# Early-fusion block on one core: one set of row statistics for two layer norms in a row, reordered attention bodies, and pair loads placed ahead of three weight loads

## The reference, cut to what matters

```python
h = tok(x)                                  # 32 images: 36 patches of 768 -> layer norm -> 192 -> layer norm, + class row
h = concat([h, txt], axis=1)                # 37 + 128 = 165 rows of 192
h = h + linear_attention(layernorm(h))      # no softmax
h = h + ffn(layernorm(h))                   # plain layer norm, then inside ffn:

def ffn(x):
    h = ln(x, g1, b1); qkv = h @ in_w.T + in_b            # a second layer norm right on the first
    x = x + softmax(q k^T / 4, 12 heads) v @ out_w.T + out_b
    x = x + gelu(x @ mlp_w1 + b1) @ mlp_w2 + b2
    xm = ln(x, g2, b2); top-2 of 4 experts by a gate; return x + weighted experts(xm)
```

## Time and profile before

| | |
|---|---|
| median of 3 runs | 1307.76 us (1306.62 to 1310.7) |
| the profiled execution, its own time | 1298.35 us |
| its span, first to last instruction | 1296.3 us |
| mean granted TensorE clock | 0.968 |
| busy: PE, DVE, ACT, POOL | 92%, 69%, 57%, 33% |
| instructions | 27864 |

### The profile page before, as it was taken

One profiled execution on the slowest core, in us unless ns is written; L12 is line 12 of the kernel. 1 busy time (PEld: TensorE's weight loads), 2 busy tenths in 40 slices (PEclk: granted clock), 3 DMA queues, 4 the chain that ended last, 5 costly groups with the idle time before them and its releaser, 6 DMA issues.

```text
span 1296.3 us, 27864 instructions
## 1 busy us (share of the span) xinstructions
PE 1191.5 (92%) x9709; PEld 1015.5 (78%) x9709; DVE 897.8 (69%) x2492; ACT 740.1 (57%) x1717; POOL 422.9 (33%) x418
## 2 busy tenths in 40 slices
PE   8885999898998999989998899999999999999994
PEld 7774777676776777777777689998988889989994
DVE  4764566766667667676667677778678876777673
ACT  4462565555655566545556665455566667667662
POOL 3511010101111010110101016787657655455544
PEclk8997999999999999999999999999999999999998
DMA  5156111212012120121220343444576767766662
GB/s 208 56 145 182 52 34 32 58 51 58 21 45 58 51 58 14 53 58 51 57 54 17 129 107 69 88 88 111 142 220 164 183 162 173 188 163 156 173 167 29
DMA packets 98554, 127.23 MB, mean 98 GB/s; under 512 B 9735, under 2 KB 90504, under 8 KB 94768
## 3 DMA queue, kind: packets, MB, share of 16 engines
q1 hardware_dynamic: 74911, 105.24, 26.9%
q0 software_dynamic: 23568, 21.06, 10.6%
HBM read 72.49 MB, written 53.72 MB: 97 GB/s over the span
## 4 chain that ended last, share of the span: by engine, by line
PE 56%; DVE 16%; issue 11%; POOL 6%; DMA 4%; SPq 3%; ACT 3%; DVEq 0%; POOLq 0%; ACTq 0%
PE PS L1863 45%; PE PS L1866 11%; DMA out<-YO,ids 3%; POOL out L891 2%; POOL expert_rows L854 2%; DVE K L1393 2%; DVE st L1293 2%; DVE XA L1304 2%; ACT GF L1177 1%; SPq L605 1%; SPq L583 1%; DVE H L1348 1%; DVE CNT L1422 1%; DVE ZS L1363 1%; DVE mv L1296 1%
## 5 line engine op out<-in xcount | busy, mean ns | idle before, releaser
L1863 PE MATMUL PS<-w2r,GH 128*120 (+1 forms) x828 | 247.6, 362 | 2.3 <-DVE GL L1588 1.1
L749 POOL TENSOR_TENSOR rs<-ve,minus_half 128x3 f32<-128x3 f32 x48 | 41.0, 854 | 535.8 <-DVE ve L1298 535.8
L891 POOL DMA_INDIRECT out<-YO,ids x94 | 162.6, 1730 | 143.7 <-DVE flag L1804 62.9
L1863 PE MATMUL PS<-w2r,GL 128*120 (+1 forms) x828 | 208.0, 251 | 0.0
L934 ACT ACTIVATE PX<-PS,nb 128x165 f32<-128x165 f32 x576 | 176.6, 416 | 39.1 <-DVE nb L1381 37.7
L1177 ACT ACTIVATE GF<-PS,b1c 128x480 f32<-128x480 f32 (+1 forms) x216 | 137.4, 637 | 82.5 <-PE PS L1863 79.7
L1863 PE MATMUL PS<-XH,w1r 128*128 128x480 f32 (+1 forms) x432 | 168.9, 393 | 6.1 <-ACT GF L1177 3.2
L1866 PE MATMUL PS<-ident,PX 128*128 128x128 f32 x864 | 136.5, 290 | 34.7 <-DVE PT L1386 27.9
L1386 DVE COPY PT<-PS 128x384 f32<-128x384 f32 x144 | 80.1, 556 | 115.0 <-PE PS L1866 114.0
L1866 PEld LDWEIGHTS PS<-ident,PX 128*128 128x128 f32 x864 | 97.3, 145 | 73.3 <-DVE PT L1386 31.5
L1863 PEld LDWEIGHTS PS<-w2r,GH 128*120 128x120 f32 x828 | 150.2, 181 | 5.7 <-DVE GL L1588 4.0
(11 more groups left out here) (292 smaller groups left out, 2327.5 us busy)
## 6 DMA issues: line engine op xcount, KB each, us to landing
w1r<-expert_w_parts SPq DMA_DIRECT2D x25, 1536.0 KB, 7.4
expert_rows<-empty SPq DMA_DIRECT2D x45, 369.4 KB, 5.6
RT<-expert_rows SPq DMA_DIRECT2D x22, 369.4 KB, 3.9
X<-x_scratch SPq DMA_DIRECT2D x11, 360.0 KB, 4.0
out<-X POOLq DMA_DIRECT2D x11, 360.0 KB, 5.6
H<-in_txt SPq DMA_DIRECT2D x16, 192.0 KB
out<-H SPq DMA_DIRECT2D x16, 192.0 KB
x_scratch<-X SPq DMA_DIRECT2D x16, 192.0 KB
```

Source lines behind the costliest of these rows:

```text
L749: nc.gpsimd.tensor_tensor(rs[:, k - 1, 0:n], ve[:, k - 1, 0:n], eps_half[:, 0:n], ALU.pow).then_inc(rstd_ready[k], 1)
L891: nc.gpsimd.indirect_dma_start(out[:, :], bass.IndirectOffsetOnAxis(ap=ids[:, i, t:t + 1], axis=0), YO[:, i % 2, t, :], None, bounds_check ...
L1863: return nc.tensor.matmul(o, l, r, start=start, stop=stop)
```

## The change

It has three parts. **Statistics**: U's own are not taken any more. `lin_out` computes two values from H1's variance v: `ve[3] = v + eps`, and `ve[4] = v (1 + eps) + eps^2`, which is (v + eps) times (v / (v + eps) + eps); POOL raises both in one instruction of six columns, and `z_out` makes Z from H1 directly, ahead of U (`u_out`). **Order**: the bodies' instructions on PE, ACT and DVE stand in a new order; the same 18 groups are copied by the same engines. **Loads**: `h1_store(1)` moves up on SP, behind `load_raw(1)`.

```diff
@@ sync @@
-        for f in range(NF):
+        load_raw(0)
+        load_raw(1)
+        sp.wait_ge(token_stored[1], 16 * (PTILES - 2))
+        h1_store(1, True)
+        for f in range(2, NF):
             load_raw(f)
...
         fill(0)
         fill(PAIRS - 2)
-        sp.wait_ge(token_stored[1], 16 * (PTILES - 2))
-        h1_store(1, True)
@@ gpsimd: rstd and body @@
+            cols = slice(k - 1, k if k == 3 else k + 1)
+            n = 3 * (cols.stop - cols.start)
...
             residual(i, first)
             if lin:
-                rstd(i + 1, 4, 3)
-                rstd(i + 1, 5, 3)
+                rstd(i + 1, 4)
@@ scalar: body @@
             exps(i, 0)
+            probsT(i, 1)
             xaT(i + 1)
             exps(i, 1)
-            probsT(i, 1)
             lin_y(i + 1, 0)
+            lin_y(i + 1, 1)
             probsT(i, 3)
             exps(i, 2)
-            lin_y(i + 1, 1)
...
             lin_m(i + 1)
+            exps(i, 4)
             probsT(i, 9)
-            exps(i, 4)
...
             probsT(i, 15)
+            contextsT(i, 0)
             probsT(i, 17)
-            contextsT(i, 0)
@@ vector: lin_out, u_stats -> u_out, z_out, body @@
-            stats(j, 4, lambda t: H1[:, t, :], 3)
-
-        def u_stats(j, first):
+            for t in range(3):
+                last = nc.vector.bn_stats(st[:, 3, t, :], H1[:, t, :])
+            steps.link_aggregate(last, pad[:, 0:1])
+            for t in range(3):
+                last = nc.vector.bn_aggr(mv[:, 3, t, :], st[:, 3, t, :])
+            steps.link(last)
+            ts(ve[:, 4, :], mv[:, 3, :, 1], 1.0 + EPS, EPS * EPS, ALU.mult, ALU.add)
+            ts(ve[:, 3, :], mv[:, 3, :, 1], EPS, None, ALU.add).then_inc(var_ready[4], 1)
+
+        def u_out(j, first):
             if not first:
                 dve.wait_ge(ub_ready, j)
             normed(j, 4, lambda t: H1[:, t, :], lambda t: U[:, t, :], 3).then_inc(u_ready, 1)
-            dve.wait_ge(u_ready, j + 1)
-            stats(j, 5, lambda t: U[:, t, :], 3)
...
-            normed(j, 5, lambda t: U[:, t, :], lambda t: Z[:, t, :], 3).then_inc(z_ready, 1)
+            dve.wait_ge(rstd_ready[4], j + 1)
+            for t in range(3):
+                last = ts(Z[:, t, :], H1[:, t, :], mv[:, 3, t, 0:1], rs[:, 4, t:t + 1], ALU.subtract, ALU.mult)
+            last.then_inc(z_ready, 1)
```

More of the change, by code:

```diff
@@ L101 @@
 CONST_FIRST = KP * D + D
+ON_ACT = (1, 3, 5, 7, 9, 11, 13, 15, 17)
 PTILES = B * NPATCH // P
@@ L374, in build_program @@
     pool_step = sem("pool_step")
-    var_ready = {k: sem(f"var_ready{k}") for k in (3, 4, 5)}
-    rstd_ready = {k: sem(f"rstd_ready{k}") for k in (3, 4, 5)}
+    var_ready = {k: sem(f"var_ready{k}") for k in (3, 4)}
+    rstd_ready = {k: sem(f"rstd_ready{k}") for k in (3, 4)}
     xn_ready = sem("xn_ready")
@@ L472, in token_bank, with copies_up_to @@
         return 5 if t == PTILES - 1 else 2 + t % 2
+    def copies_up_to(g, on_act):
+        return sum((k in ON_ACT) == on_act for k in range(g + 1))
     def probT_views(g):
@@ L761, in body @@
             if lin and not first:
-                rstd(i + 1, 3, 3)
+                rstd(i + 1, 3)
             residual(i, first)
             if lin:
-                rstd(i + 1, 4, 3)
-                rstd(i + 1, 5, 3)
+                rstd(i + 1, 4)
         prstd(0)
@@ L776, in _ @@
         yrstd(1)
-        rstd(0, 3, 3)
+        rstd(0, 3)
         patch_tokens(1)
@@ L793, in _ @@
         patch_tokens(4)
-        rstd(0, 4, 3)
+        rstd(0, 4)
         yrstd(5)
         positions(6)
-        rstd(0, 5, 3)
         patch_tokens(5)
@@ L805, in _ @@
         patch_tokens(7)
-        rstd(1, 3, 3)
+        rstd(1, 3)
         yrstd(8)
@@ L1449, in body @@
             maxima(i, 1)
+            maxima(i, 2)
             probsT(i, 2)
-            maxima(i, 2)
             maxima(i, 3)
@@ L1458, in body @@
             maxima(i, 5)
-            lin_out(i + 1)
             probsT(i, 12)
             probsT(i, 14)
-            u_stats(i + 1, False)
+            lin_out(i + 1)
             probsT(i, 16)
             z_out(i + 1)
+            u_out(i + 1, False)
             contextsT(i)
@@ L1530, in _ @@
         token_stats(5)
-        u_stats(0, True)
+        z_out(0)
+        u_out(0, True)
         token_stats(6)
-        z_out(0)
         patch_stats(8)
@@ L1543, in _ @@
         before = steps.base + steps.k
-        N_STEPS = 9
+        N_STEPS = 7
         with dve.Fori(1, PAIRS - 2) as i:
@@ L1946, in scores_may_follow, with copied @@
             pe.wait_ge(prob_ready, i * 6 + u - 1)
+        def copied(i, g):
+            if g in ON_ACT:
+                pe.wait_ge(probT_act_ready, i * len(ON_ACT) + copies_up_to(g, True))
+            else:
+                pe.wait_ge(probT_dve_ready, i * (18 - len(ON_ACT)) + copies_up_to(g, False))
         def transpose_probs(i, *gs):
@@ L1953, in transpose_probs @@
                 if g >= 2:
[L1954 to L1957, removed]
+                    copied(i, g - 2)
                 for slot, col in enumerate((0, PXW - NTXT, NTXT)):
@@ L2070, in contexts_T @@
                 pe.wait_ge(v_ready, i + 1)
-                pe.wait_ge(probT_act_ready, i * 9 + 6)
-                pe.wait_ge(probT_dve_ready, i * 9 + 6)
+                for g in range(12):
+                    if all((k in ON_ACT) != (g in ON_ACT) for k in range(g + 1, 12)):
+                        copied(i, g)
             for c in range(3):
[L2074 to L2077, removed]
+                if b == 1:
+                    copied(i, 12 + c)
+                    copied(i, 15 + c)
                 bank, col = (2 * b, c * D) if c < 2 else (1, b * D)
@@ L2132, in body @@
             scores(i, 4)
-            scores(i, 5)
             transpose_probs(i, 8)
             lin_m(i + 1)
+            scores(i, 5)
             transpose_probs(i, 9)
+            lin_tokens(i + 1, 0)
             transpose_probs(i, 10)
-            lin_tokens(i + 1, 0)
-            lin_tokens(i + 1, 1)
             transpose_probs(i, 11)
             transpose_probs(i, 12)
+            lin_tokens(i + 1, 1)
             transpose_probs(i, 13)
             transpose_probs(i, 14)
+            contexts_T(i, 0)
             transpose_probs(i, 15)
-            contexts_T(i, 0)
             transpose_probs(i, 16)
```

5 lines of the change are left out of this document (3 added, 2 removed).

## The result

| | kernel before | changed kernel |
|---|---|---|
| median of the runs | 1307.19 us (1306.28 to 1310.7, 4 runs) | 1269.66 us (1267.94 to 1270.14, 4 runs) |
| ratio, 95% interval | | 0.9706 [0.9685, 0.9726] |
| profiled execution, its span | 1298.35, 1296.3 | 1270.14, 1268.4 |

What follows compares the result with a forecast made beforehand. PE, busy 92%, was taken as the bound, losing time in waits and lowered clock. Second body -17.1, the 13 behind -17.4, setup -1 gave 1262.9 from 1298.35; 8 us of median offset made 1271, range 1261 to 1289.

Steps and rivals of the forecast that it cites:

- The loads: Second body: the patch tokens' load comes in time with 4 us margin, so the whole gap goes; second body -17.1 us.
- The body: One loop body at full clock: waits of 2.2 us go, 2.1 come, so 39.93 becomes 39.7 us.
- each us of it is on the path: POOL's six-column power, taken as 1.46 us, delays Z directly; at its bounds 0.86 and 3.05 the body is 39.1 or 41.3.
- The clock: PE's clock in the bodies holds, as the longest new wait is 0.8 us; this decides a third of the gain.
- The setup: Before the first body: U(0)'s statistics leave the way to Z(0) and the last patch block, 0 to 1.4 us, taken as -1.
- The sum: Whole kernel on the profiled execution's scale: 1298.35 - 35.5 = 1262.9 us.
- The 9.4 us: Whole kernel: the earlier median, 1307.76, lay 9.4 us above the profiled execution, unexplained; 8 were carried, giving 1271.
- 1 (the clock still falls): Bodies: new waits of 0.8 and 0.7 together still lower PE's clock; bodies of 41.2, 1292 us; chance 0.17.
- 2: Bodies: the clock's falls have nothing to do with the wait, ten of 13 bodies still cost 1.5 more; 1287 us; chance 0.08.
- 3: Second body: the load is still late behind eight large transfers on SP, so 13.5 us stay; 1285 us; chance 0.05.
- 4: Bodies: POOL's six-column power costs 3.05 us and the clock falls in all; bodies of 42.8, 1316 us; chance 0.04.
- 5 (bodies of 39.0): Bodies: ACT's waits don't come and the context's copies are hidden; 1262 us; chance 0.12.

Runs made afterwards that it cites:

- run 1: Kernel before with only SP's order changed, H1's store and the loads moved up: 1280.7 us beside 1297.3, ratio 0.9877.
- run 6: Changed kernel with POOL's six-column power issued twice, the first result unread: 1280.4 us, beside 1259.9 for the changed kernel and 1296.0 for the kernel before.
- run 3: Changed kernel (early loads, one set of statistics) with the old order on PE, ACT and DVE: 1279.2 us, kernel before 1297.3, ratio 0.9871.
- run 4: Changed kernel (early loads, new order) with U's own statistics and power put back: 1304.0 us, kernel before 1297.3, ratio 1.0052.
- run 5: Kernel before with ten unread identity transposes in PE's wait for group 12's copy: 1281.8 us beside 1296.0, ratio 0.9883.
- runs 8: Changed kernel with two added unread powers ahead of Z, one of six columns and one of three: 1300.9 us, kernel before 1295.1, ratio 1.0034.
- run 7: Kernel before with three unread identity transposes in PE's wait for group 12's copy: 1292.0 us beside 1295.1, ratio 0.9965.
- late U: Changed kernel with U written later, in its own pair's body behind maxima(2): 1241.2 us, kernel before 1295.1, ratio 0.9582.

## Why the prediction was right, and where it was not

**The loads** (right). I had the store at about 95 and the load done in time with a margin of 4; H1 was out at 90.8. The second body lost 17.53, forecast 17.1; run 1 gives 16.6 for it alone. That X's store, late by the fills, is hidden held too.

**The body** (right, 39.57 for 39.7). Term by term: the wait for group 12's copy gone, as said; Z 0.45 for 0.8; the context's copies 0.56 for 0.7; ACT 0.46 and 0.25 for 0.35 and 0.25. POOL's power of six columns took 1.33 for 1.46: 0.16 a column was right, but counted from the 0.855 of three columns and not from the 1.14 of four. Run 6 bears out the statement "each us of it is on the path" (1.29 for 1.33). "U's statistics were under POOL and PE time" is shown by run 3, and what I did not see by run 4: the new order without the single statistics is worse than the old order.

**The clock** (right in result, by too simple a reason). It holds at 1.00 in every body. That is 533.55 - 13 x 39.93 = 14.5 us of the 19.2 in the 13 bodies; the other 4.7 are 0.36 in each from shorter waits. Run 5 has 14.2 by the clock alone. "The fall follows the one long wait" is shown by run 5, and runs 8 and 4 agree: no long wait, no falls in the bodies. A long wait does not always bring one (ten of 13 bodies in the kernel before). That 0.8 was short enough was a guess without a row behind it, and in part luck: behind waits of 1.5 to 1.8 us the clock fell in most bodies of run 7 and in none of run 6. The Trainium skill, "TensorE: Matmul & The Clock Gate", section on the clock gate, warns of idle gaps longer than these. The rows of run 7 show a fall behind 1.51 us; the measurement decides. What else decides is open. The place may: ahead of Z's transposes PE runs half a `contexts_T` of 1.89 us without a pause, ahead of group 14 three short groups with a pause of 0.25, and no run exchanged them. The moment may too: the two first bodies shown under run 7 differ in it and not in the place.

**The setup** (mis-sized). I took -1, bounded by 0 and -1.4, the time of U's statistics. The first score came 4.3 us sooner in the two profiles, and over all fourteen profiles the nine with one set of statistics have it at 61.5 to 65.5 (mean 63.2), the five with two at 64.7 to 67.4 (mean 65.9): 2.7, with up to 2.3 between an execution and its mean. This term is the one that failed: it held U's statistics alone, and little of the gain is theirs. DVE needs 3.8 us less from H1's statistics to Z(0) in the changed kernel's profile, since U and a second trip to POOL no longer stand between, but PE transposes Z(0) at 54.8 in the mean of the five and at 54.3 in that of the nine, only 0.5 sooner. From there to the first score it takes 11.0 in the mean of the five and 8.9 in that of the nine. All five have a stretch of lowered clock there; of the nine only late U has one (10.2), and the others take 8.6 to 9.0. The kernel before, and the changed kernel:
```profile
56.27:67.39 11.12, 8.77 (x40) 7.91 (x40) 6.68 (x25) 6.20 (x13) 3.77 (x9) 0.69 0.06 18
54.40:63.11 8.71, 6.15 (x42) 5.45 (x39) 6.18 (x24) 5.49 (x12) 3.77 (x9) 1.00 0.03 11
```
So most of it is a clock term that the sum put at nothing in the setup. What sets that fall off no run shows.

**The sum** (1262.9 on the profiled scale, 4.6 too high). On a chip where the second phase takes its 565, the changed kernel's profiled execution took 1258.28, 4.6 less: setup and first body 3.4 for 1 (second body from 104.05), the second body 17.5 for 17.1, from there to the last store 19.0 for 17.4, and 0.2 outside.

**The 9.4 us** (nearly the right amount, for another reason, with luck). I carried 8 of them to 1271 and supposed that part might be bodies with a lowered clock. The changed kernel's second phase was 12.7 longer in its profile, without such bodies, and the kernel before took 1295 to 1297 in the three sets of runs above, on three chips. So the changed kernel's offset was the chip's and lies in its second phase. That it lay there in the kernel before's own timed runs too is inferred from their 1307, since no profile shows them; with the changed kernel's second phase they would have taken 1311 (730.9 + 578.1 + 2.0). By the medians the changed kernel's offset is 9.7 (1269.66 - 1259.94), by its two profiled executions 11.9 (1270.14 - 1258.28), of which I carried 8. On that scale the offset was 3.9 too small and the sum 4.6 too high. The two cancelled, and that the forecast lies within 1.4 us of the result is luck.

The rivals: 1 (the clock still falls) did not come true but was the closest, as runs 8 and 4 show; 2 fell by run 5, 3 by run 1; 4 by the power of 1.33; 5 (bodies of 39.0) was not reached.

## What to carry to other kernels

Price an order together with the dependences that it was made for: here the statistics alone gave no more than 1.5 us, the order alone cost 23, and the two together gave 21. A wait of 1.5 us on TensorE can cost another 1.5 through the clock right behind it, in most turns of a loop; ten transposes of the identity in it were worth 14 us, and are a quick test of whether a fall follows from a wait. After such a change read PE's list of waits again and ask of each what stands ahead of its releaser without being needed: writing U later and giving Z its own power took another 24 us.

## What was unexpected of the hardware

- The clock fell behind a wait of 1.51 us in nine of 13 bodies at one place and held in all of them behind one of 1.74 at another, where it fell behind 2.56. At a third, behind a wait of 1.9 to 2.02 us, it fell in six profiles and held in four.
- The same code took 565 to 567 us in twelve runs on three chips and 578 in one other, with ACT idle there for up to 5.4 us at a time on something that the trace calls remote.
- The time of POOL's power grew with its columns: 0.86 us for three, 1.14 for four (120 partitions), 1.33 for six, 3.05 for sixteen (120 partitions).
